# Layer 2's mixing of groups 1 to 3 with stationary tables inside the group ahead, and its routing products behind each unit's down products

## The reference

```python
# mixing of layers 1 to 3 (numbers from 0), per sample b
agg_w = einsum('bk,koi->boi', att, weight[..., 0]); agg_b = att @ bias_k
out = einsum('boi,bih->boh', agg_w, x) + agg_b[:, :, None]
# layer 2's feed-forward part: 512 -> 1792 -> 512
h = silu(t @ W_gate.T) * (t @ W_up.T)
x = x + h @ W_down.T
# layer 3's: three experts; the first token of each sample picks two of them by its gate scores
moe_out = sum over the two of top_val * expert_out[expert of the sample]
```

## Time and profile before

| what | value |
| --- | --- |
| median of 3 runs | 780.34 us (779.86 to 783.27) |
| the profiled execution's own time | 779.9 us |
| its span, first to last instruction | 778.0 us |
| mean granted clock of TensorE | 0.985 of full speed |
| layer 2 with layer 3's routing (by the windows) | 198 to 547 us of the span |

### The profile page before, as it was taken

How to read it: one execution, slowest core, us unless ns; L and a number is a source line. 1 busy time by engine, 2 the same in 40 slices (tenths; PEclk the granted TensorE clock), 3 DMA queues, 4 the chain that set the end, 5 groups by cost and what they waited for, 6 DMA issues and landing times.

```text
span 778.0 us, 11186 instructions
## 1 busy us (share of the span) xinstructions
PE 750.6 (96%) x3644; PEld 605.1 (78%) x3660; DVE 478.1 (61%) x1039; ACT 275.6 (35%) x532; POOL 419.5 (54%) x449
## 2 busy tenths in 40 slices
PE   8999999999899999999999999899899978999997
PEld 5587788787688888888788888777688766888886
DVE  2467667778623255753477256874788888576643
ACT  6444444453432233332424243232342332333211
POOL 2756667775425432111411045778677866778870
PEclk9699999999999999999999999999999998999999
DMA  9446446544051013100331022314313211212110
GB/s 281 71 109 168 160 154 199 164 136 136 28 190 54 28 59 91 55 29 1 94 109 20 10 73 81 131 56 135 124 42 117 60 41 56 69 42 83 55 41 27
DMA packets 49335, 69.60 MB, mean 89 GB/s; under 512 B 25864, under 2 KB 26120, under 8 KB 49016
## 3 DMA queue, kind: packets, MB, share of 16 engines
q1 hardware_dynamic: 39520, 38.65, 16.7%
q0 software_dynamic: 9152, 29.69, 12.5%
q10 hardware_dynamic: 608, 0.55, 0.2%
HBM read 45.71 MB, written 17.66 MB: 81 GB/s over the span
## 4 chain that ended last, share of the span: by engine, by line
PE 79%; DVE 14%; issue 3%; ACT 3%; DVEq 1%; ACTq 0%
PE bank L2024 23%; PE bank L1881 10%; PE bank L1975 9%; PE bank L2007 8%; PE bank L1720 8%; PE bank L1654 4%; PE bank L1758 3%; PE bank L1851 2%; DVE junk L1363 2%; PE bank L1790 1%; PE bank L1986 1%; PE bank L1770 1%; PE bank L1901 1%; DVE tl L1319 1%; ACT th L957 1%
## 5 line engine op out<-in xcount | busy, mean ns | idle before, releaser
L1512 DVE TENSOR_TENSOR sil<-bank,sil 128x512 f32<-128x512 f32 x56 | 38.6, 690 | 95.2 <-PE bank L2024 95.2
L1975 PE MATMUL bank<-wda,xch 128*128 (+1 forms) x272 | 87.9, 405 | 4.3 <-DVE xcl L1537 4.3
L2024 PE MATMUL bank<-th,wgr 128*128 128x512 f32 x224 | 88.3, 394 | 2.5 <-POOL tl L563 1.8
L1881 PE MATMUL bank<-wda,hh 128*128 128x512 f32 x224 | 88.4, 394 | 0.0
L2024 PE MATMUL bank<-th,wur 128*128 128x512 f32 x224 | 87.4, 390 | 0.0
L1881 PE MATMUL bank<-wda,hl 128*128 128x512 f32 x224 | 87.3, 390 | 0.0
L2024 PE MATMUL bank<-tl,wgr 128*128 128x512 f32 x224 | 87.2, 389 | 0.0
L2024 PE MATMUL bank<-tl,wur 128*128 128x512 f32 x224 | 87.2, 389 | 0.0
L1060 ACT ACTIVATE hh<-sil 128x512 fp32r<-128x512 f32 x56 | 35.4, 632 | 109.4 <-DVE sil L1512 109.4
L790 POOL TENSOR_TENSOR raw<-raw,bias 128x512 f32<-128x512 f32 x48 | 67.1, 1397 | 4.0
L1514 DVE TENSOR_TENSOR hl<-sil,hh 128x512 fp32r<-128x512 f32 x56 | 44.7, 798 | 39.1 <-ACT hh L1060 39.1
(11 more groups left out here) (329 smaller groups left out, 1880.4 us busy)
## 6 DMA issues: line engine op xcount, KB each, us to landing
tap<-in_x_taps_dram SPq DMA_DIRECT2D x16, 260.0 KB, 3.0
xin<-in_x_rows_dram SPq DMA_DIRECT2D x16, 256.0 KB, 3.0
xd<-xo SPq DMA_DIRECT2D x16, 256.0 KB, 3.2
xc<-xd SPq DMA_DIRECT2D x16, 256.0 KB, 3.3
xres<-xd SPq DMA_DIRECT2D x4, 1024.0 KB, 5.5
xd<-xres SPq DMA_DIRECT2D x4, 1024.0 KB, 4.7
tsd<-tf SPq DMA_DIRECT2D x4, 1024.0 KB
raw<-in_w_dram POOLq DMA_DIRECT2D x16, 256.0 KB, 3.1
```

Of the source, the lines that this page charges most:

```text
L1512: v.tensor_tensor(hf[:, m % 2], p_pre[(2 * m + 1) % 3][:], sil[:, m % 2], ALU.mult).then_inc(s_hf, 1)
L1881: last = mm(p_acc[j][:], h[:, m % HSLOTS, j * P:(j + 1) * P], wda[:, m * D:(m + 1) * D], start=(m == 0 and n == 0), stop=(m == MT - 1 and ...
L1975: last = mm(bank[(p + 1) % 2][:], x, y, start=(k == 0 and n == 0), stop=(k == KT - 1 and n == 2))
L2024: last = mm(p_pre[(2 * m + b) % 3][:], w[:, (m * KT + kt) * P:(m * KT + kt + 1) * P], x[:, kt], start=(kt == 0 and n == 0), stop=(kt == KT ...
```

## The change

For groups 1 to 3, layer 2's mixing moves into units 10 to 13 of the group ahead: `cond2(s + 1, m - 10)` behind the up products of unit m makes three products of 512 columns with the table stationary, into bank 3. ACT writes them to tf as rows with a bias per partition (`rows2_out`), in the same units, and makes the high part of tiles 2 and 3 of x there; DVE makes their low parts in units 11 and 12. At the boundary PE then transposes tf with 16 products of 128 columns (`features_t`), ACT takes the high parts of the features from PSUM (`t_hi_p`), and DVE all four low parts (`t_lo_p`). The bias columns of layer 2 are loaded by SP with the tables of layer 3's form (four more small loads), and the bias rows of groups 1 to 3 are not loaded. Group 0 is as before.

Second, in every unit of layer 2 the down products move ahead of `router_sums`, `class_rows`, `ranks` and `permutation`. The remaining edits (two pairs of semaphores shared, counts) move nothing.

```diff
@@ -362,9 +362,9 @@
                     rows = slice(CH * b, CH * (b + 1))
                     dst = ag1[rows] if l == 0 else ag23[rows, (l - 1) * TILES:l * TILES]
                     sp.dma_start(dst, mixed[b, :, 0:AGW].rearrange("t (i o) -> i t o", i=CH)).then_inc(d_tab, 16)
-                    if l != 1:
-                        sp.dma_start((bcol3 if l else bcol1)[rows], mixed[b, :, AGW:AGB].rearrange("t o -> o t"),
-                                     allow_slow_non_contiguous=True).then_inc(d_tab, 16)
+                    sp.dma_start(bcol23[rows, (l - 1) * TILES:l * TILES] if l else bcol1[rows],
+                                 mixed[b, :, AGW:AGB].rearrange("t o -> o t"),
+                                 allow_slow_non_contiguous=True).then_inc(d_tab, 16)
...
@@ -410,8 +410,6 @@
 
             def load_next(c):
 
-                sp.wait_ge(s_tf, c * KT)
-                load_bias(c)
                 sp.wait_ge(s_xcld, c * 2)
                 load_xc(c * GT, 0)
                 load_xc(c * GT, 1)
...
@@ -722,7 +720,6 @@
             split3(0)
             split3(1)
             constants()
-            t_lo(1)
             for s in range(1, LAST):
                 pool.wait_ge(s_cond, (s + 1) * GT)
                 diag_full(TILES + (s - 1) * GT)
@@ -731,7 +728,6 @@
                     x3_lo(s - 1, j)
                 pool.wait_ge(s_c3, s * GT)
                 ahead(s + 1)
-                t_lo(s + 1)
...
+
+            def t_hi_p(c):
+                for kt in range(KT):
+                    act.wait_ge(s_tr2, (c - 1) * KT + kt + 1)
+                    nc.scalar.activation(th[:, kt], p_pre[kt][:], ACT.Copy).then_inc(s_th, 1)
+
+            def rows2_out(c, j):
+
+                act.wait_ge(s_cond, c * GT + j + 1)
+                if j == 0 and c == 1:
+                    act.wait_ge(s_tlp, 2)
+                    act.wait_ge(s_tld, 2)
+                    act.wait_ge(d_tab, 16 * 6 * BPT)
+                elif j == 0:
+                    act.wait_ge(d_tsd, 16 * (c - 1))
+                    act.wait_ge(s_lg, (c - 1) * GT)
+                nc.scalar.activation(tf[:, j], bank[3][:], ACT.Identity,
+                                     bias=bcol23[:, c * GT + j:c * GT + j + 1]).then_inc(s_te2, 1)
...
@@ -1015,16 +1029,15 @@
             def rows_out(c, k):
 
                 act.wait_ge(s_c3, c * GT + k + 1)
-                act.wait_ge(d_tab, 16 * 5 * BPT)
+                act.wait_ge(d_tab, 16 * 6 * BPT)
                 j = GT - 1 - k if c == LAST else k
                 if c < LAST:
-                    act.wait_ge(s_tlp, 2 * (c + 2))
-                    act.wait_ge(s_tld, 2 * (c + 2))
+                    act.wait_ge(s_tr2, (c + 1) * KT)
...
-            def boundary(c):
-                x_hi(c, 2, c * 32 + 32)
-                x_hi(c, 3, c * 32 + 32)
-                t_hi(c)
 
             for s in range(GROUPS):
                 c = s - 1
@@ -1073,8 +1081,12 @@
                             ahead(s + 1)
                         else:
                             diag_hi(2 * LAST + 1)
+                    if s < LAST and m >= MT - GT:
+                        rows2_out(s + 1, m - (MT - GT))
+                        if m < MT - 2:
+                            x_hi(s + 1, m - (MT - GT) + 2, (s + 1) * 32 + 32)
                 if s < LAST:
-                    boundary(s + 1)
+                    t_hi_p(s + 1)
 
...
+            def t_lo_p(c):
+                for kt in range(KT):
+                    dve.wait_ge(s_th, c * KT + kt + 1)
+                    v.tensor_tensor(tl[:, kt], p_pre[kt][:], th[:, kt].bitcast(F32), ALU.subtract).then_inc(s_tld, 1)
...
@@ -1525,9 +1540,10 @@
                         order_one(0)
                     if s == LAST and m == 11:
                         indices(0)
+                    if s < LAST and MT - GT < m < MT - 1:
+                        x_lo(s + 1, (m - (MT - GT) + 1,))
                 if s < LAST:
-                    x_lo(s + 1)
-                    t_rows(s + 1)
+                    t_lo_p(s + 1)
                     residual(s, s_down, (s + 1) * MT)
...
+            def cond2(c, j):
+
+                pe.wait_ge(s_gl, 2 * c)
+                if j < 2:
+                    pe.wait_ge(s_xclp, c * 2 + j + 1)
+                else:
+                    pe.wait_ge(s_xcld, c * 2 + j - 1)
+                if j:
+                    pe.wait_ge(s_te2, (c - 1) * GT + j)
+                elif c == 1:
+                    pe.wait_ge(s_tf, KT)
+                else:
+                    pe.wait_ge(s_clsd, c - 1)
+                for k, (w, y) in enumerate(parts((bdh[:, j], bdl[:, j]), (xch[:, j % 2], xcl[:, j % 2]))):
+                    last = mm(bank[3][:], w, y, start=(k == 0), stop=(k == 2))
+                last.then_inc(s_cond, 1)
+
+            def features_t(c):
+
+                pe.wait_ge(s_te2, c * GT)
+                for kt in range(KT):
+                    for j in range(GT):
+                        last = nc.tensor.transpose(p_pre[kt][:, j * P:(j + 1) * P], tf[:, j, kt * P:(kt + 1) * P], ident[:])
+                    last.then_inc(s_tr2, 1)
+
             def wait_t(c, kt):
 
-                pe.wait_ge(s_tld if kt % 2 else s_tlp, c * 2 + kt // 2 + 1)
-
+                if c:
+                    pe.wait_ge(s_tld, 2 + (c - 1) * KT + kt + 1)
+                else:
+                    pe.wait_ge(s_tld if kt % 2 else s_tlp, kt // 2 + 1)
...
@@ -1891,7 +1932,7 @@
                 pe.wait_ge(s_gl, min(2 * c + 3, 2 * GROUPS))
                 pe.wait_ge(s_x3l, n + 1)
                 if c < LAST:
-                    pe.wait_ge(s_tf, (c + 2) * KT)
+                    pe.wait_ge(s_tld, 2 + (c + 1) * KT)
@@ -2030,6 +2071,10 @@
                             linear1(TILES - 1)
                     if s >= 1 and 2 <= m < 6:
                         cond3(c, m - 2)
+                    if s < LAST and m >= MT - GT:
+                        cond2(s + 1, m - (MT - GT))
+                    if m >= LAG2:
+                        down2(s, m - LAG2, s == 0)
                     if s >= 1 and m == 7:
                         router_sums(c)
                     if s >= 1 and m == 8:
@@ -2038,11 +2083,9 @@
                         ranks(0)
                     if s == LAST and m == 11:
                         permutation(0)
-                    if m >= LAG2:
-                        down2(s, m - LAG2, s == 0)
                 if s < LAST:
                     pe.wait_ge(s_hf, (s + 1) * MT)
-                    cond(s + 1)
+                    features_t(s + 1)
                     for m in range(MT - LAG2, MT):
                         down2(s, m)
```

More of the change, by code:

```diff
@@ L277, in build @@
         s_cvw, s_gas, s_w0s, s_w0l, s_lbs = (sem(f"s_{n}") for n in "cvw gas w0s w0l lbs".split())
-        s_bias, s_m1, s_g1, s_lm, s_ex, s_at, s_att, s_atc, s_mb, s_ag, s_agc = (
-            sem(f"s_{n}") for n in "bias m1 g1 lm ex at att atc mb ag agc".split())
+        s_bias, s_m1, s_g1, s_ex, s_at, s_att, s_atc, s_ag, s_agc = (
+            sem(f"s_{n}") for n in "bias m1 g1 ex at att atc ag agc".split())
         s_sw, s_wqf, s_wqr, s_wqt, s_wqc = (sem(f"s_{n}") for n in "sw wqf wqr wqt wqc".split())
@@ L291, in build @@
         d_bias, d_xres, d_st = sem("d_bias"), sem("d_xres"), sem("d_st")
-        s_xch, s_xclp, s_xcld, s_gf, s_gh, s_gl, s_cond, s_tf, s_th, s_tld, s_tlp, s_res = (
-            sem(f"s2_{n}") for n in "xch xclp xcld gf gh gl cond tf th tld tlp res".split())
+        s_xch, s_xclp, s_xcld, s_gf, s_gh, s_gl, s_cond, s_tf, s_th, s_tld, s_tlp, s_res, s_tr2, s_te2 = (
+            sem(f"s2_{n}") for n in "xch xclp xcld gf gh gl cond tf th tld tlp res tr2 te2".split())
         d_w2, d_raw = sem("d_w2"), sem("d_raw")
@@ L399, in _ @@
                     load_xc(0, 1)
-                    load_bias(0)
+                    load_bias()
             sp.wait_ge(s_xch, 2)
@@ L583, in step @@
                 if t == 8:
-                    pool.wait_ge(d_tab, 16 * 5 * BPT)
+                    pool.wait_ge(d_tab, 16 * 6 * BPT)
                     diag_full(0)
@@ L625, in _ @@
             x1_bias(TILES - 1)
-            t_lo(0)
+            t_lo()
             x_after_1(TILES - 2)
@@ L995, in _ @@
             diag_hi1(TILES - 1)
-            t_hi(0)
+            t_hi()
             mixed1(TILES - 1)
@@ L1026, in rows_out @@
                 nc.scalar.activation(tf[:, j], bank[2 if c == LAST else 3][:], ACT.Identity,
-                                     bias=bcol3[:, c * GT + j:c * GT + j + 1]).then_inc(s_te, 1)
+                                     bias=bcol23[:, TILES + c * GT + j:TILES + c * GT + j + 1]).then_inc(s_te, 1)
             def route_exp(c):
@@ L1161, in _ @@
             chain.link(v.tensor_reduce(attm[:, 0, :], att[:], AX.X, ALU.max))
-            v.tensor_tensor(att[:], att[:], rows(0), ALU.subtract).then_inc(s_lm, 1)
+            v.tensor_tensor(att[:], att[:], rows(0), ALU.subtract).then_inc(s_at, 1)
             dve.wait_ge(s_ex, 1)
@@ L1308, in x_lo, with t_rows @@
```

(30 more changed lines are left out.)

18 lines of the change are left out of this document (9 added, 9 removed).

## The result

The changed kernel took 770.63 us (median of 5 runs, 769.79 to 774.32), the kernel before 780.34 us in its 5 (779.86 to 783.27). The execution that the profiler took of it was the longest of the five (774.32 us, span 772.5) and had the lowest mean clock (0.979, the others 0.986 to 0.987), so its trace has to be compared stretch by stretch and not by its end. What the prediction calls layer 4 is layer 3 of the sections ahead of it, the layer of the experts.

A forecast was written before the change was run, and what follows sets the result against it. PE, busy 96% of the span, was taken as the bound. 779.9 - 5.3 (Term A) - 3.25 (Term B) = 771.35 us; with 0.44 for the median 771.8, stated as 771.7, range 769.7 to 775.0.

The forecast's parts named there:

- Term A: Layer 2's three group boundaries: table products and transposes replace 48 small mixing products, gaining 5.3 us (bounds 3.8 to 5.6).
- The stretch I had put at 9.2 us: PE from unit 11's first down product to the next group's first up product, in the changed kernel.
- the charge of 0.1 us for a wait on the evictions: At each boundary, PE's transposes would wait about 0.1 us for ACT's eviction of tf tile 3.
- the slots of 0.226 and 0.11: PE cost in us, counted by starts: 0.226 per product of 512 columns, 0.11 per transpose of 128 columns.
- The chain behind the transposes: At each boundary, high and low parts of the features finish 1.7 us before PE asks, covered by 16 down products.
- rival 4: Groups 1 and 2: late x tile loads hold up ACT in unit 10, and so PE; 783 us and more, 3%.
- Term B: Group 3, routing products behind down products: gain 3.45 us, less 0.2 at layer 4's first gather, 3.25 (bounds 1.85 to 4.5).
- the first wait: PE's 2.22 us wait before unit 7's router sums in group 3; down(5) fills it, putting PE 1.85 us ahead.
- The second wait: PE's wait of about 2.3 us before unit 11's permutation products in group 3, forecast to shrink to 0.9.
- Rival 2: Group 3's wait before the permutation products stays, DVE's order step running longer beside POOL's splits: 773.2 us, 11%.
- rival 3: PE's lead from group 3 is given back at layer 4's first gather, landing late: 775.0 us, 6%.
- the clock should stay at the top in group 3: Sign to look for in the changed kernel's profile: PE's granted clock stays at the top there; no size given.

The follow-up runs named there:

- experiment 5: Changed kernel with the transposes moved behind down(12) and down(13), so nothing covers the high and low parts: 772.53 us, ratio 0.9903.
- experiment 3: Kernel before with only the down products put ahead of the routing products: all units 777.36 us; units 7 and 8 only 775.01; all other units 779.45.
- experiments 1 and 2: experiment 1, then its kernel with products nobody reads put into both PE waits of group 3: 128 columns wide 775.34 us, 512 columns wide 772.62.
- the filled run: Kernel of experiment 1 with 8 products of 512 columns, whose result nobody reads, in each of group 3's two PE waits: 772.62 us, ratio 0.9884.
- Experiment 3's last kernel: Kernel before with the down products ahead of the routing products in all units but 7 and 8: 779.45 us, ratio 0.9995.
- experiment 1: Changed kernel with the tables and transposes alone, the down products put back behind the routing products: 777.95 us, ratio 0.9951.

## Why the prediction was right, and where not

**Term A** was to be 5.3 us and measured 1.28 + 2.00 + 1.92 + 0.68 = 5.9 (the last is the wait for the features that is gone from group 3's first unit; units 0 to 2 of that group took 14.05 us before and 13.37 after). The stretch I had put at 9.2 us is 9.01. The step that failed is the charge of 0.1 us for a wait on the evictions, and most of the 0.1 for the change of lengths; the slots of 0.226 and 0.11 held to the hundredth. The chain behind the transposes is covered, as worked out (1.7 us foreseen, 1.6 there), and experiment 5 shows what it costs uncovered: 0.8 us a boundary. ACT, SP and the x tiles cost nothing that shows: in groups 1 and 2 no row has ACT waiting for an x tile, as rival 4 would have it.

**Term B** was to be 3.45 less 0.2 and measured 4.0 up to unit 12 (72.97 us from the group's start before, 68.28 now, less unit 0's 0.68), then 3.35 at the token transposes. The mechanism held: the first wait is filled, PE's lead lets DVE start unit 10's rows earlier. Its number came out by luck: sizes were off and cancelled. The second wait vanished instead of shrinking to 0.9, as the operations of DVE met other splits of POOL. The router sums started 0.3 us later than forecast, counted from the group's start (43.47 us, where 43.85 less 0.68 was to be). And behind unit 12 0.66 us and not 0.2 went back, 0.54 of them at the gather: its rows reached PE 3.5 us after the issue began (529.72 to 533.21; 4.6 in experiment 3), where the forecast had taken 2.6 to 3.3 from the loads. Rival 2 had the right worry, DVE beside POOL, with the wrong sign; rival 3 came in small.

**What the prediction did not have** is the clock. It took a wait for its length, and the two terms for independent. Alone they give ratios of 0.9951 and 0.9952, together 0.9871: 0.97% in the sum against 1.29%, a gap that the intervals could still hold. For the tables experiments 1 and 2 show a reason: behind the two waits, 0.3 us longer in that profile, the clock falls, and the filled run gets the gain back. Both kernels compared in the forecast had a clock of 1.00 in group 3's profile, so the sum by rows came out right. That was in part luck: the prediction said that the clock should stay at the top in group 3, and worked out nothing for what it does behind a wait. Why the routing part alone gives no more than units 7 and 8 do is not settled. Its group 3 is 2.54 us shorter, but its layer 3 took 235.96 us in the profile, 2.2 more than before, and the clock that layer 3 lacked, summed as above, was 8.5 us where before had 5.1 and the kernel with units 7 and 8 alone 6.8. Experiment 3's last kernel lacked 8.5 too. One profile of each cannot tell whether their other runs did, and the runs of the routing part scatter from 773.0 to 781.3 us.

**The number** 771.7 against 770.63: 0.7 us of it are the two terms (9.2 instead of 8.55). The rest, 0.4, is less than the scatter.

## What to carry to other kernels

Count products by their starts and not by their bars; sixteen transposes at 0.11 us against 48 mixing products at 0.12 was a sum that held to 0.2 us a boundary. A wait of PE like these of 2 to 3 us can be worth more than its length, since the clock can fall behind it. It is worth trying independent wide products there: in group 3 they gave about 5 us, in layer 3 they kept the clock up behind one wait and the total did not fall. And do not judge a change that leaves such a wait by the profile of one execution. Before a wait is closed by a lead, look at what the waiting engine's operations share with others, and at what the lead runs into next, here a gather that another engine issues on its own pace.

## What was not expected of the hardware

- TensorE's granted clock fell to half behind waits of 2.5 us in a stretch that is dense otherwise, and not behind 2.2 us in the kernel before; in layer 3 it fell behind waits of 1.3 and 3.0 us in most profiles, and at the start of layer 2 behind 1.41 and 0.42 us in one of fourteen. 16 products of 128 columns in a wait (1.90 us) did not always keep it up, 8 of 512 columns (1.98 us) did in both places.
- The same kernel scatters, and in part with its mean clock. Over 27 runs of the kernel before, the time goes from 783.2 us at a mean clock of 0.978 to 773.5 at 0.991; but another run at 0.991 took 778.1. That the clock of its longer runs falls in group 3 is argued from experiment 1, not shown: only one execution of it was profiled.
- A DVE operation on 64x3 numbers in the order step takes 0.14 us, or 1.2 where it has two SBUF inputs and meets a POOL split.
- PE's value loads with little queued work ahead of them left it idle for 1.2 us more, put down to "issue" (2.71 us against 1.47).
